# Moving 6 of 16 drive products of a state-space scan from VectorE to ScalarE, with PE transposes

## The reference, cut to what matters

```python
dt = softplus(dt_low @ W_dt + b_dt)
dA = exp(dt[..., None] * A[None, None])         # A = -exp(A_log)
dB = dt[..., None] * Bc[:, :, None, :]
s  = da_t * state + db_t * u_t                  # scan over the 2048 tokens
y  = einsum('blms,bls->blm', states, Cc)
y  = (y + x_m * D) * silu(z)
return y @ W_out
```

## Time and profile before

| what | value |
|---|---|
| time, median of 3 runs | 1027.47 us (1027.14 to 1028.28) |
| the profiled execution's own time | 1018.8 us |
| its span | 1016.7 us |
| mean granted TensorE clock over the span | 0.754 of 2.4 GHz |
| stretch of the 128 scan steps | 49.6 to 552.3 us of the span |

### The profile page before, as it was taken

One profiled execution on the slowest core, in us unless ns is written; L12 is line 12 of the kernel. 1 busy time (PEld: TensorE's weight loads), 2 busy tenths in 40 slices (PEclk: granted clock), 3 DMA queues, 4 the chain that ended last, 5 costly groups with the idle time before them and its releaser, 6 DMA issues. The chain is left out here.

```text
span 1016.7 us, 10897 instructions
## 1 busy us (share of the span) xinstructions
PE 731.2 (72%) x3551; PEld 478.0 (47%) x3551; DVE 705.3 (69%) x1321; ACT 432.2 (43%) x609; POOL 521.5 (51%) x412
## 2 busy tenths in 40 slices
PE   4779978899788997887977663689711870189770
PEld 2355545645456454564655332656611720166550
DVE  7699989999898999999997778422103596812220
ACT  1556935469355595543541554033101273013220
POOL 4057656566575665756665310178760040037864
PEclk9968975799757999578565775589765975559895
DMA  4234433334343343333431533023333006013332
GB/s 126 86 105 144 145 126 137 132 117 151 109 144 126 125 145 128 143 126 129 150 134 63 187 93 88 12 47 43 40 29 91 2 0 181 1 26 46 43 37 21
DMA packets 60067, 96.03 MB, mean 94 GB/s; under 512 B 6392, under 2 KB 40224, under 8 KB 60000
## 3 DMA queue, kind: packets, MB, share of 16 engines
q1 hardware_dynamic: 48192, 85.67, 25.8%
q0 software_dynamic: 11264, 8.66, 6.5%
q10 hardware_dynamic: 560, 1.05, 0.4%
HBM read 81.99 MB, written 13.37 MB: 94 GB/s over the span
## 5 line engine op out<-in xcount | busy, mean ns | idle before, releaser
L280 POOL TENSOR_TENSOR product<-state,c_all 128x1024 f32<-128x1024 f32 x128 | 302.8, 2366 | 218.5 <-DVE state L484 200.4
L613 PE MATMUL m_psum<-ident,product 128*128 128x128 f32 x1024 | 181.2, 334 | 3.7 <-POOL product L280 3.7
L613 PEld LDWEIGHTS m_psum<-ident,product 128*128 128x128 f32 x1024 | 144.7, 172 | 65.0 <-issue 48.4
L470 DVE TENSOR_TENSOR m_psum<-m_psum,dtu 128x1024 f32<-128x1024 f32 x128 | 155.0, 1211 | 20.8 <-PE m_psum L628 20.7
L366 ACT ACTIVATE decay<-dt,decay_rate 128x1024 f32<-128x1024 f32 x128 | 144.3, 1146 | 49.4 <-DVE state L484 45.7
L484 DVE TENSOR_TENSOR_SCAN state<-decay,carry,m_psum 128x1024 f32<-128x1024 f32 x64 | 150.1, 2345 | 4.4
L628 PE MATMUL m_psum<-b_split,pick_r 64*128 64x512 f32 x256 | 116.6, 543 | 48.1 <-DVE state L484 47.6
L484 DVE TENSOR_TENSOR_SCAN state<-decay,m_psum 128x1024 f32<-128x1024 f32 x64 | 146.2, 2285 | 4.4
L703 POOL DMA_INDIRECT f_got<-f_table,f_tokens x64 | 61.8, 966 | 148.9 <-DVE f_tokens L1069 121.4
L628 PEld LDWEIGHTS m_psum<-b_split,pick_r 64*128 64x128 f32 x256 | 47.7, 232 | 111.4 <-DVE state L484 86.5
L1236 ACT ACTIVATE f_hidden<-f_psum,shared_b_T 128x512 f32<-128x512 f32 x64 | 44.0, 688 | 108.7 <-PE f_psum L1274 108.7
(11 more groups left out here) (182 smaller groups left out, 980.1 us busy)
## 6 DMA issues: line engine op xcount, KB each, us to landing
c_all<-c_dram SPq DMA_DIRECT2D x128, 512.0 KB, 3.6
f_table<-f_rows SPq DMA_DIRECT2D x2, 2176.0 KB, 10.3
X<-in_L_attn_a_x SPq DMA_DIRECT2D x4, 512.0 KB, 7.4
f_w_raw<-in_L_ffn_fc2s SPq DMA_DIRECT2D x1, 2048.0 KB, 15.5
between<-f_f SPq DMA_DIRECT2D x1, 2048.0 KB, 8.8
X<-between SPq DMA_DIRECT2D x4, 512.0 KB, 6.9
out<-f_f SPq DMA_DIRECT2D x1, 2048.0 KB, 8.9
f_got<-f_table,f_tokens POOLq DMA_INDIRECT x64, 2.5
```

The lines of the kernel that those rows point to most:

```text
L280: pool.tensor_tensor(product[:, n % RING, :], state[:, n % RING, :], c_all[:, n % RING, :], ALU.mult).then_inc(product_ready, 1)
L470: dve.tensor_tensor(pair(n), pair(n), dtu[:, k, :].rearrange("p (a t) -> p a t", t=BANK), ALU.mult).then_inc(drive_ready, 1)
L613: last = pe.matmul(psum[:, Y + i // BT, i % BT * P:(i % BT + 1) * P], product[:, n % RING, i * P:(i + 1) * P], ident[:], start=False, stop ...
```

## The change

In steps whose state s is 5, 7, 9, 11, 13 or 15 (48 of 128) DVE no longer makes the drive and PE no longer broadcasts B. ACT makes the drive with tokens on the partitions, so that B is a scale per partition: eight activations of 128x128 per step, four of them after its work of step n-3 and four after its work of step n-2. PE turns the eight blocks into the PSUM pair. For that PE also makes dtu with tokens on partitions once per half chunk (piece "turn", eight transposes, two copies on ACT) and B with tokens on partitions once per chunk (piece "bT", eight small matmuls, one copy on ACT). The steps at which u and z are done move a little. `BY_POOL` is empty, so POOL makes none.

```diff
+        BY_ACT, BY_POOL = (5, 7, 9, 11, 13, 15), ()
+        EARLY = 3
...
-            out = [("v", g, 1, t, (3,)) for t in range(TB)]
+            out = [("turn", 0, 0, t, (0,)) for t in range(TB)] if g == 0 else []
+            out += [("v", g, 1, t, (3,)) for t in range(TB)]
...
+            out += [("turn", g, 1, t, (9,)) for t in range(TB)]
-            u_at = ((8, 8, 9, 9), (10, 11, 11, 12), (13, 14, 14, 15), (16, 17, 17, 18))
-            z_at = (10, 13, 16, 19)
+            u_at = ((10, 10, 11, 11), (12, 12, 13, 13), (14, 14, 15, 15), (16, 17, 17, 18))
+            z_at = (11, 13, 16, 19)
...
+                out += [("bT", g + 1, 0, 0, (26,))]
                 out += [("again", g + 1, 0, t, (28,)) for t in range(TB)]
+                out += [("turn", g + 1, 0, t, (30,)) for t in range(TB)]
...
         START += [("mixed", 0, 0, t, ()) for t in range(TB)]
+        START += [("bT", 0, 0, 0, ())]
...
@@ scalar, take()
+                elif kind == "bT":
+                    act.wait_ge(bT_summed, g + 1)
+                    if g >= 2:
+                        act.wait_ge(drive_turned, made(PERIOD * (g - 1), "act", "pool"))
+                    act.copy(b_T[:, g % 2].rearrange("p i s -> p (i s)"), bank[:, 0:CT * NS]).then_inc(bT_ready, 1)
+                elif kind == "turn":
+                    act.wait_ge(dtu_turned, count_of(*piece[:4]))
+                    if g:
+                        act.wait_ge(drive_turned, made(PERIOD * (g - 1) + NS * (k + 1), "act", "pool"))
+                    act.copy(dtu_T[:, k, BT * t:BT * (t + 1), :].rearrange("p i c -> p (i c)"),
+                             bank).then_inc(dtuT_ready, 1)
+
+            def drive_by_act(n, first, end):
+
+                g, k, s = place(n)
+                turn = made(n, "act", "pool")
+                act.wait_ge(bT_ready, g + 1)
+                act.wait_ge(dtuT_ready, count_of("turn", g, k, (end - 1) // BT))
+                if first == 0 and turn >= 2:
+                    act.wait_ge(drive_turned, turn - 1)
+                for i in range(first, end):
+                    act.activation(drive_T[:, turn % 2, i], dtu_T[:, k, i], ACT.Copy,
+                                   scale=b_T[:, g % 2, i, s:s + 1]).then_inc(act_drive, 1)
...
+                for ahead, first in ((EARLY, 0), (EARLY - 1, CT // 2)):
+                    if n + ahead < STEPS and maker(n + ahead) == "act":
+                        drive_by_act(n + ahead, first, first + CT // 2)
...
@@ vector
-                dve.wait_ge(drive_ready, n + 1)
+                if maker(n) == "dve":
+                    dve.wait_ge(drive_ready, made(n + 1, "dve"))
+                else:
+                    dve.wait_ge(drive_turned, made(n + 1, "act", "pool"))
...
-                force(n)
+                if maker(n) == "dve":
+                    force(n)
...
@@ tensor
+                elif kind == "bT":
+                    pe.wait_ge(b_ready, TB * (g + 1))
+                    for j in range(CT):
+                        last = pe.matmul(out[:, j * NS:(j + 1) * NS],
+                                         b_split[B_AT:P, g % 2, j * P:(j + 1) * P], pick_r[B_AT:P, :, 0],
+                                         start=True, stop=True)
+                    last.then_inc(bT_summed, 1)
+                elif kind == "turn":
+                    pe.wait_ge(dtu_ready, KB * g + k + 1)
+                    for j in range(BT):
+                        at = t * BANK + j * P
+                        last = pe.transpose(out[:, j * P:(j + 1) * P], dtu[:, k, at:at + P], ident[:])
+                    last.then_inc(dtu_turned, 1)
...
+                    if maker(n) == "dve":
+                        for t in range(TB):
+                            last = pe.matmul(pair(n)[:, t, :], pick_r[B_AT:P, s, :],
+                                             b_split[B_AT:P, g % 2, t * BANK:(t + 1) * BANK],
+                                             start=True, stop=True)
+                        last.then_inc(b_bcast, 1)
+                    else:
+                        if maker(n) == "act":
+                            pe.wait_ge(act_drive, CT * made(n + 1, "act"))
+                        else:
+                            pe.wait_ge(pool_drive, made(n + 1, "pool"))
+                        for i in range(CT):
+                            last = pe.transpose(pair(n)[:, i // BT, i % BT * P:(i % BT + 1) * P],
+                                                drive_T[:, made(n, "act", "pool") % 2, i], ident[:])
+                        last.then_inc(drive_turned, 1)
```

More of the change, by code:

```diff
@@ L97, in mamba @@
         c_all = sb("c_all", [P, RING, CHUNK])
+        dtu_T = sb("dtu_T", [P, KB, CT, P])
+        b_T = sb("b_T", [P, NCHUNK, CT, NS])
+        drive_T = sb("drive_T", [P, 2, CT, P])
         y_T = sb("y_T", [P, CT, P])
@@ L138, in mamba @@
         b_bcast = sem("b_bcast")
+        bT_summed = sem("bT_summed")
+        bT_ready = sem("bT_ready")
+        dtu_turned = sem("dtu_turned")
+        dtuT_ready = sem("dtuT_ready")
+        act_drive = sem("act_drive")
+        pool_drive = sem("pool_drive")
+        drive_turned = sem("drive_turned")
         c_loaded = [sem(f"c_loaded{r}") for r in range(RING)]
@@ L156, in mamba, with maker, made @@
         TAKE_Y = LAG + 1
+        BY_ACT, BY_POOL = (5, 7, 9, 11, 13, 15), ()
+        EARLY = 3
+        def maker(n):
+            s = n % NS
+            return "act" if s in BY_ACT else "pool" if s in BY_POOL else "dve"
+        def made(n, *by):
+            return sum(maker(i) in by for i in range(n))
         def beside(g):
             last = g + 1 == CHUNKS
-            out = [("v", g, 1, t, (3,)) for t in range(TB)]
+            out = [("turn", 0, 0, t, (0,)) for t in range(TB)] if g == 0 else []
+            out += [("v", g, 1, t, (3,)) for t in range(TB)]
             if g:
@@ L193, in count_of @@
         def count_of(kind, g, k, t):
-            if kind in ("v", "again", "z", "back"):
+            if kind == "bT":
+                return g + 1
+            if kind in ("v", "again", "z", "back", "turn"):
                 return (g * KB + k) * TB + t + 1
@@ L268, in dt_times_u, with drive_by_pool @@
                                    ALU.mult).then_inc(dtu_ready, 1)
+            def drive_by_pool(n):
+                g, k, s = place(n)
+                turn = made(n, "act", "pool")
+                pool.wait_ge(bT_ready, g + 1)
+                pool.wait_ge(dtuT_ready, count_of("turn", g, k, TB - 1))
+                if turn >= 2:
+                    pool.wait_ge(drive_turned, turn - 1)
+                pool.tensor_tensor(drive_T[:, turn % 2], dtu_T[:, k],
+                                   b_T[:, g % 2, :, s:s + 1].broadcast_to([P, CT, P]),
+                                   ALU.mult).then_inc(pool_drive, 1)
             for n in range(STEPS):
@@ L275, in _ @@
                     dt_times_u(g + 1, 0)
+                if n + EARLY < STEPS and maker(n + EARLY) == "pool":
+                    drive_by_pool(n + EARLY)
                 pool.wait_ge(c_loaded[n % RING], 16 * (n // RING + 1))
@@ L466, in force @@
                 g, k, s = place(n)
-                dve.wait_ge(b_bcast, n + 1)
-                if s == 0:
-                    dve.wait_ge(dtu_ready, KB * g + k + 1)
+                dve.wait_ge(b_bcast, made(n + 1, "dve"))
+                dve.wait_ge(dtu_ready, KB * g + k + 1)
                 dve.tensor_tensor(pair(n), pair(n), dtu[:, k, :].rearrange("p (a t) -> p a t", t=BANK),
@@ L526, in wait_free @@
                     pe.wait_ge(added, count)
+                elif kind == "bT":
+                    pe.wait_ge(bT_ready, count)
+                elif kind == "turn":
+                    pe.wait_ge(dtuT_ready, count)
                 elif kind == "mixed":
```

## The result

The changed kernel takes 1002.88 us (median of 4 runs, 1000.04 to 1003.34) against 1027.45 us (4 runs) before: 24.6 us less, a ratio of 0.975 with a 95% interval of 0.9735 to 0.9765. The forecast was 1007 us. Measured again later the two took 1003.08 and 1028.07, a ratio of 0.9756.

What follows compares the result with a forecast made beforehand. DVE was taken as the bound, PE not far behind. Gained 61.9 us less 42 given back is net 20: 1018.8 to 998.8, plus 8.7 is 1007.5; forecast 1007, own range 985 to 1022, whole range 972 to 1045.

Steps and rivals of the forecast that it cites:

- its own sign: PE's granted clock over the scan stage: expected 0.70 to 0.77, the prediction wrong if it leaves 0.65 to 0.85.
- The gain of 61.9 us: Scan steps: DVE loses 48 products at 1.29 us, 61.9 us, if the next scan can start at once.
- PE at the low clock, 23 us given back: Pairs of one DVE and one ACT step at 1.2 GHz: 26 of 48 lose 0.9 us each, 23 us.
- PE's pieces: Added transposes and small matmuls in PE's queue ahead of the next drive: delay DVE 8 us in all (0 to 20).
- ScalarE, 8 + 9 us: ScalarE's drive activations delay DVE: 8 us behind `soften` (1.2 us, 7 times), 9 us (0 to 18) in steps 11 to 22.
- The start, 1 us: Before the scan: "bT" puts a wait, eight matmuls and a copy ahead of v, costing 1 us.
- The 6.6 us for y turned back: DVE's waits, read from the profile before: 6.6 us for y turned back, beside 20.7 us for PE's broadcast.
- The sum: Whole kernel: gained 61.9, given back 49 less 7 for stalls that fall together, 42; net 20 us.
- The 8.7 us from the profiled execution to the median: Whole kernel before: the median shown stands 8.7 us above the profiled execution of 1018.8 us, so 998.8 becomes 1007.5.
- All is covered: Rival, chance 0.12: denser PE gets the full clock nearly throughout and ACT's slack suffices; 970 us.
- The clock falls: Rival, chance 0.23: transposes replace matmuls on PE, its clock falls; at 0.62 a chunk takes 132 us, the kernel 1052.
- ScalarE becomes the bound: Rival, chance 0.13: drive activations at 0.41 to 0.48 us bound the scan stage at 462 to 490 us; 1015 if dearer.

Runs made afterwards that it cites:

- the run with z beside u: The changed kernel with z at steps 11, 13, 15, 18 instead of 11, 13, 16, 19, so all four z share a step with a u: 997.75 us, ratio 0.971.
- the wide activations: The version with z beside u, ScalarE making a drive by two activations of 512 columns instead of eight of 128, result wrong: 982.95 us, ratio 0.967.

## Why the prediction was right, step by step, and where by luck

The time was forecast well and one mechanism was not: by its own sign, a granted clock of the stage outside 0.65 to 0.85, the prediction failed on the clock.

- **The gain of 61.9 us** was 54.7 us of DVE's busy time; with a gap of 0.08 us that goes with each product it is 58.5. Two scans on end take 4.63 to 4.70 us.
- **PE at the low clock, 23 us given back**, failed as it was put. I had a granted clock of 0.70 to 0.77, it was 0.88, and outside the u stretches DVE's waits for PE grew by only 0.6 us. A pair that is one broadcast and 24 transposes, spaced by 5.8 us, kept PE at 2.4 GHz in the last half chunk, where the kernel before had 0.60: after, it had 0.91. The window of the scans alone in the last half chunk, in the columns of the earlier trace rows, is

```profile
471.00:528.00 57.00, 40.97 (x18) 0.91 0.41 146
```

I had weighed the rule of the Trainium skill (TensorE: Matmul & The Clock Gate, Part 4: PE-mode transpose), that transposes do not engage the full rate, and taken as agreeing with it. The run with extra transposes (fp32) contradicts both readings (0.91, plain steps at 1.00).
- **PE's pieces** made up for it by a term that I had mis-sized. I counted a u, z, mixed, v or again unit as one pass of 512 columns (0.87 us low); each is two matmul records, 0.86 us even at the full clock. In the u stretch PE then needs 7.73 us for a pair that I had at 3.9 plus u. DVE's waits for PE rose by 14.7 us in all, of these 14.1 in the u stretches (some of it at the low clock, as above). The added pieces themselves, 8 us and 1 us of start in the forecast, cost 7.0 us in the run that has only them. The sum of 148 us a chunk in the rival on the clock was too low by 28 for the same reason.
- **ScalarE, 8 + 9 us**: the activation took 389 ns (0.38 estimated), 0.317 each in a row (0.29). ScalarE's busy time was 390.6 us (391 forecast). Behind `soften` DVE waited 1.71 us where I had 1.2; all waits for decays are 7.3 us, and those for the split of B, which I had not counted, 5.6. The load in steps 11 to 22 cost 5 to 6 us by the run with z beside u, through PE's queue.
- **The start, 1 us**, was 2.8 and 3.7 us in two profiles. "bT" leaves PE idle before it, and the xn transposes behind it ran at the low clock: 20 in 4.53 us at 43.07, where the kernel before did 20 in 2.40 us.
- **A misreading.** The 6.6 us for y turned back, counted among the waits of the scans, lie behind the last scan (that product starts at 558.71 us). The idle time of the scans is 20.7 us for PE and nearly all of the rest the gap of 0.08 us at each product. Nothing in the sum used it.
- **The sum.** Net 20 forecast, 24.6 measured. Given back: 25.7 us more idle time in the stretch and 3.7 before it. That the total is near is luck: it rests on two errors that cancel, the low clock, overrated, and the u units, underrated. The 8.7 us from the profiled execution to the median were right to add; they lie behind the scans.
- **The rivals.** "All is covered" had its clock come true and not its time. "The clock falls" is refuted in its mechanism. "ScalarE becomes the bound" is refuted by the activation's 0.389 us and by the wide activations.

Open is why the extra matmuls held the clock less than the extra transposes, and how DVE's waits for PE outside the u stretches, 17.6 us, divide between the stretches at 1.2 GHz that remain, PE's waits for ScalarE and the order of PE's queue.

## What to carry to other kernels

When one engine sheds work, sum up the next one stretch by stretch, in matmul records and not in calls: here PE was the bound, mostly at its full clock, for some 9 of 32 steps, while averages said that it had room. Added PE work can raise PE's clock (transposes, 0.77 to 0.91) or do so much less (the narrow matmuls, 0.83), so charge it at neither clock without a run. And when two kinds of table functions alternate on ScalarE, try putting them into the same step: one line gave 5 us.

## What the hardware showed unexpectedly

- PE transposes of 128x128 in fp32 kept PE at 2.4 GHz in plain steps that ran at 1.2 GHz without them (stage 0.77 to 0.91); matmuls of 64 partitions x 512 columns, of about equal PE time (1.03 us for the four added, 0.97 for the eight transposes, at 2.4 GHz), left plain steps at 1.2 GHz with PE busy throughout (stage 0.83).
- An fp32 matmul of 512 columns and 128 partitions is two records and 0.86 us at 2.4 GHz; the broadcast's, whose operands are stored as fp32r, are one record each.
- The layers behind the scan, equal in all versions, took 462 to 467 us in the traces where the kernel before had a median of 1017 us, and 474 to 477 where it had 1027 to 1028. The scans do not differ so: two nearly equal versions, one on either kind of chip, ended theirs at 518.2 and 518.7 us.
